# Two-buffered own rows and x rows in the second GCN edge stage of a four-layer graph network

## What is computed

```python
def gcn_conv(x, W, b, src, dst, n_nodes):      # src, dst with self-loops
    xw = x @ W
    deg = segment_sum(ones, dst)
    dis = rsqrt(deg)
    norm = dis[src] * dis[dst]
    return segment_sum(norm[:, None] * xw[src], dst) + b

h = relu(layernorm(x))
x = x + gcn_conv(relu(gcn_conv(h, W1, b1)), W2, b2)
h = relu(layernorm(x))                          # then the next layer
```

## Time and profile before

| | us |
|---|---|
| median of three runs | 5211.01 |
| lowest and highest run | 5206.4 and 5215.85 |
| profiled execution, its own time | 5226.53 |
| span of the profiled execution | 5224.8 |
| mean granted TensorE clock | 0.920 |
| busy in the span: TensorE / its weight loads | 75% / 63% |
| busy in the span: VectorE / GpSimd / ScalarE | 67% / 65% / 53% |

### The profile page before, as it was taken

The page is one execution under the profiler, slowest core; times in us unless marked ns, Lnnn a source line. Parts: engine busy times, 40 slices in busy tenths (PEclk is TensorE's granted clock), DMA queues, the critical chain, the costliest instruction groups (busy, mean ns, idle before and its releaser), DMA issues. The chain is left out here.

```text
span 5224.8 us, 117088 instructions
## 1 busy us (share of the span) xinstructions
PE 3910.9 (75%) x27481; PEld 3315.7 (63%) x27481; DVE 3497.0 (67%) x12527; ACT 2786.6 (53%) x7212; POOL 3413.1 (65%) x3998
## 2 busy tenths in 40 slices
PE   2888888888977698779999888665864966640176
PEld 1666666666866576778888777565764865640165
DVE  5888888886668766876666799327635833865433
ACT  2777777773434333656666688323522632430186
POOL 2666666665767576767567474575676667567577
PEclk9999999998988899999999999897997999875599
DMA  2776666664568676874334465794795788489443
GB/s 68 197 211 213 212 212 213 210 207 128 151 173 229 185 206 189 242 209 118 107 105 117 116 175 155 220 284 116 185 285 162 165 258 261 113 255 392 145 140 108
DMA packets 1087203, 971.64 MB, mean 186 GB/s; under 512 B 113214, under 2 KB 845974, under 8 KB 1087036
## 3 DMA queue, kind: packets, MB, share of 16 engines
q1 hardware_dynamic: 992956, 805.13, 50.6%
q0 software_dynamic: 94080, 164.48, 13.0%
HBM read 488.42 MB, written 484.70 MB: 186 GB/s over the span
## 5 line engine op out<-in xcount | busy, mean ns | idle before, releaser
L1093 POOL DMA_INDIRECT G<-table,idx_all x1568 | 1543.8, 985 | 758.8 <-issue 496.7
L1093 POOL DMA_INDIRECT G<-table,idx_l x588 | 603.8, 1027 | 291.5 <-issue 178.4
L1765 PE MATMUL PS<-G,S 128*128 (+1 forms) x2352 | 405.9, 290 | 27.8 <-DMA G<-table,idx_all 16.0
L1765 PE MATMUL PS<-CR,LO 97*128 97x128 f32 x2352 | 335.7, 288 | 67.8 <-ACT CR L2168 66.7
L1765 PEld LDWEIGHTS PS<-G,S 128*128 128x128 f32 x2352 | 351.0, 203 | 47.0 <-issue 29.0
L1765 PEld LDWEIGHTS PS<-S,G 128*128 128x128 f32 x1960 | 253.7, 195 | 168.2 <-issue 150.7
L1765 PEld LDWEIGHTS PS<-CR,LO 97*128 97x128 f32 x2352 | 303.6, 202 | 80.5 <-ACT CR L2168 79.5
L2168 ACT ACTIVATE G<-G 128x128 f32<-128x128 f32 x784 | 322.1, 483 | 60.4 <-issue 55.5
L1765 PE MATMUL PS<-S,G 128*128 128x128 f32 x1960 | 284.8, 287 | 92.6 <-DMA G<-table,idx_all 42.3
L1765 PE MATMUL PS<-G,FS 128*65 (+1 forms) x1764 | 276.4, 291 | 91.9 <-DMA G<-table,idx_all 52.8
L1765 PE MATMUL PS<-WX,OT 128*128 128x130 f32 (+1 forms) x2168 | 304.8, 285 | 36.9 <-ACT OT L2168 35.8
(11 more groups left out here) (381 smaller groups left out, 11146.4 us busy)
## 6 DMA issues: line engine op xcount, KB each, us to landing
table<-G SPq DMA_DIRECT2D x392, 256.0 KB, 3.4
table<-RO SPq DMA_DIRECT2D x271, 260.0 KB, 3.5
table<-RO SPq DMA_DIRECT2D x245, 256.0 KB
XIN<-xrows SPq DMA_DIRECT2D x196, 256.0 KB
table<-OWN SPq DMA_DIRECT2D x147, 260.0 KB
OWN<-table SPq DMA_DIRECT2D x139, 256.0 KB, 3.6
F<-table SPq DMA_DIRECT2D x132, 256.0 KB, 3.5
S<-table SPq DMA_DIRECT2D x100, 260.0 KB
```

What stands on the lines that cost most here:

```text
L1093: g.indirect_dma_start(G[:, t, 0:w], None, TAB[s], bass.IndirectOffsetOnAxis(ap=idx[:, t:t + 1], axis=0)).then_inc(gat[t % 4].sem, 16)
L1765: return nc.tensor.matmul(o, l, r, start=start, stop=stop)
```

## The change

In `C2` the product of own rows and `dis2` moves from VectorE to ScalarE (`scale_own`, four ACTIVATEs, one for each tile), two quads ahead. TensorE adds the scaled rows to the sums by four matmuls with the identity in `carries`. VectorE adds x to the sums straight from PSUM and drops the steps `own` and `comb`. x rows get a second buffer (`UT`, free in this stage) and are loaded two quads ahead; SP loads own rows after `agg` of the quad that used the buffer, in place of `comb`.

```diff
+        XINS = (XIN[:, :, :], rowwise(UT[:, :]))
...
-        scaled_own = steps("scaled_own", {"C1": ("own",)})
+        scaled_own = steps("scaled_own", {"C1": ("own",), "C2": ("own",)})
...
-            "C2": ("own", "comb", "x", "stats", "aggr", "rs", "nb"),
+            "C2": ("x", "stats", "aggr", "rs", "nb"),
...
                 def load_own(n, h):
-                    used, step = {"S1": (own_turned, "oT"), "C1": (agg, "t0"), "GZ": (agg, "t0")}.get(kind, (vd, "comb"))
+                    used, step = {"S1": (own_turned, "oT"), "C1": (agg, "t0"), "C2": (agg, "t0"), "GZ": (agg, "t0")}.get(kind, (vd, "comb"))
...
+                def load_x_h(n, h):
+                    if not isinstance(n, int) or n > 1:
+                        sp.wait_ge(vd.sem, vd.at(s, n - 2, "x"))
+                    else:
+                        sp.wait_ge(vd.sem, vd.at(s, 0))
+                    sp.dma_start(XINS[h], quad_rows(X_SRC[s], quad(n))).then_inc(xin_h[h].sem, 16)
...
                     if kind in own[h].order and at < LAST - 1:
                         load_own(n + 2, h)
+                    if kind == "C2" and at < LAST - 1:
+                        load_x_h(n + 2, h)
...
                 if kind == "C2":
-                    dve.wait_ge(own[h].sem, own[h].at(s, turn, "rows"))
-                    ins = v.tensor_tensor(own4, own4, wide(dis2[:, ds(Q4, 4)], D), ALU.mult)
-                    step(s, n, ins, "own")
                     aggregated(s, n)
-                    step(s, n, v.tensor_tensor(U4, A, own4, ALU.add), "comb", s3)
                     x_free(s, n, h, turn)
-                    step(s, n, v.tensor_tensor(XOUT[kind][h], U[:, :, :], XIN[:, :, :], ALU.add), "x", s2)
+                    step(s, n, v.tensor_tensor(XOUT[kind][h], A, XINS[h], ALU.add), "x", s3, s2)
...
-                if KINDS[s] == "GZ":
-                    pe.wait_ge(hself.sem, hself.at(s, n, "own"))
+                if KINDS[s] in ("C2", "GZ"):
+                    if KINDS[s] == "C2":
+                        pe.wait_ge(scaled_own.sem, scaled_own.at(s, n, "own"))
+                    else:
+                        pe.wait_ge(hself.sem, hself.at(s, n, "own"))
                     for i in (3, 2, 1, 0):
                         mm(sums_of(h, i), ident[:, :], OWNS[h][:, i, 0:D], False, False)
...
+            def scale_own(s, n, h, m):
+                Q4 = n * (-4) + 4 * LAST
+                act.wait_ge(own[h].sem, own[h].at(s, m, "rows"))
+                for j in range(4):
+                    row = OWNS[h][:, j, 0:D]
+                    i = f(row, row, ACT.Copy, scale=dis2[:, ds(Q4 + j, 1)])
+                i.then_inc(scaled_own.sem, 1)
...
                 if kind == "C2":
                     ahead(3, 2, 1)
+                    if not isinstance(n, int) or n < LAST - 1:
+                        scale_own(s, n + 2, h, m + 1)
                     sqrts(s, n)
                     ahead(0)
                     act.wait_ge(st_t.sem, st_t.at(s, n))
                     scaled(s, n, ACT.Relu, XOUT[kind][h])
...
+                if kind == "C2":
+                    scale_own(s, 0, 0, 0)
+                    scale_own(s, 1, 1, 0)
```

More of the change, by code:

```diff
@@ L328, in gnn_program @@
                      (QUADS + 1 - b) // 2) for b in (0, 1)]
-        xin = steps("xin", {k: ("rows",) for k in ("C2", "S2", "LB", "GZ")}, 16)
+        xin = steps("xin", {k: ("rows",) for k in ("S2", "LB", "GZ")}, 16)
         eas = steps("eas", {k: ("attr",) for k in ("LA", "LB")}, 16)
@@ L404, in gnn_program @@
         own_g = [Steps(sem(f"own_g{b}"), {"GA": ("rows",)}, 16, 0, KINDS, (QUADS + 3 - b) // 4) for b in range(4)]
+        xin_h = [Steps(sem(f"xin_h{b}"), {"C2": ("rows",)}, 16, 0, KINDS, (QUADS + 1 - b) // 2) for b in (0, 1)]
         st_g = [Steps(sem(f"st_g{b}"), {"GA": ("table",)}, 16, 0, KINDS, (QUADS + 1 - b) // 2) for b in (0, 1)]
@@ L966, in _ @@
                     load_own(1, 1)
+                if kind == "C2":
+                    load_x_h(0, 0)
+                    load_x_h(1, 1)
                 if kind in xin.order:
@@ L1580, in x_free @@
             def x_free(s, n, h, turn):
-                dve.wait_ge(xin.sem, xin.at(s, n, "rows"))
+                if KINDS[s] == "C2":
+                    dve.wait_ge(xin_h[h].sem, xin_h[h].at(s, turn, "rows"))
+                else:
+                    dve.wait_ge(xin.sem, xin.at(s, n, "rows"))
                 if not isinstance(n, int) or n > 1:
@@ L1906, in tile @@
                     else:
-                        used = "x" if kind == "GZ" else "comb"
+                        used = "comb" if kind == "S2" else "x"
                         pe.wait_ge(vd.sem, vd.at(s, n, used) - 2 * len(vd.order[kind]))
@@ L2396, in out_rows @@
                     f(RO[:, :, 0:D], bank(7), ACT.Copy).then_inc(ad.sem, 1)
[L2398 to L2404, removed]
                 def body_c1(n, h, m):
@@ L2412, in body_c1 @@
                     if among(n, 3):
-                        scale_own(n + 3, 1 - h, m + 1 + h)
+                        scale_own(s, n + 3, 1 - h, m + 1 + h)
                 def body_s1(n, h, m):
```

## The result

The changed kernel took **5317.43 us** in the median of four runs (5311.49 to 5319.91); the kernel before took 5210.2 beside it (four runs, 5206.4 to 5215.85). The ratio is **1.0202, 95% interval 1.0189 to 1.0215**: slower by 107 us. Forecast were 5326 us and a range of 5283 to 5375.

A forecast was written before the change was run, and what follows sets the result against it. VectorE's chain was taken to bound C2 at 5.88 us a quad; the changed loop takes 8.40. 46 quads give +115.9 us, start 1.9 later, last quads 2.4 saved: +115.4 on the median 5211.01, so 5326 us, range 5283 to 5375.

The forecast's parts named there:

- The ring: C2's closed chain per quad: GN store, own-rows load, four ACTIVATEs, root, norm, next store; forecast 8.40 us instead of 5.88.
- The fixed part, 4.60: Each C2 quad's loop without the load's landing: 0.02 and 0.84 to load issue, ACTIVATEs 1.28, root to norm 0.81, norm 1.65.
- L, 3.8: In C2, time from issue of the own-rows load to the start of the ACTIVATE waiting for it, taken as 3.8 us.
- the third rival: C2's own-rows load comes sooner as the longer quad thins traffic: L 2.85 to 3.4, about 5296 us; chance 0.11.
- the second rival: C2's own-rows load comes as late as the sage stage's x rows: L 4.2 to 4.86, about 5360 us; chance 0.15.
- The start: C2 up to quad 0's store: one load without a store ahead and eight more TensorE passes, 1.9 us later.
- The tail: C2's last two quads, which load nothing: without VectorE's L1594 and L1597 they save 2.4 us, at most 2.8.
- The sum: C2's total: 115.9 us for 46 quads, 1.9 later at the start, 2.4 saved at the end, together +115.4 us.
- What was to be seen: Signs in C2's changed profile: stores 8.0 to 8.8 us apart, VectorE below 50%, ScalarE waiting about 3.5 us a quad.
- Hidden after all: C2's own-rows load is hidden and GpSimd's gathers become the bound: 22 to 25 us saved, 5187 us; chance 0.06.
- TensorE as the bound: In C2, TensorE's eight added passes at a lower clock set the pace: about 5350 us, up to 5377; chance 0.08.

The follow-up runs named there:

- Run 1: Changed kernel, with SP issuing the load of own rows one turn earlier, ahead of the store of GN: 5208.35 us, 0.9945 of the kernel before.
- run 2: Changed kernel, SP's order kept, with ScalarE scaling the own rows behind the norm instead of ahead of its root: 5215.17 us, 0.9957 of the kernel before.
- run 5: Changed kernel, with SP issuing the load of own rows last in its turn, behind load and store of x: 5398.65 us, 1.035 of the kernel before.
- run 3: Changed kernel without TensorE's four identity matmuls in C2, own rows scaled but not added: 5334.54 us, 1.02 of the kernel before.
- run 8: Changed kernel with the two buffers of own rows exchanged, even quads into F, odd into OWN: 5319.73 us in one run.

## Why the prediction was right, and where its sizes were not

*The ring.* Right. The prediction said that a load with two quads of lead becomes a round trip inside each quad, since it stands in SP's order behind a store that waits for the norm. Run 1 takes that one thing away and the loss with it, and 0.55% more; run 2 cuts the ring at ScalarE and does the same; run 5 delays the load's issue by 1.18 us and its landing by 0.30, and the quad grows by 1.48.

*The fixed part, 4.60.* It measured 4.46: 8.20 less the mean landing of 3.74. The sum took the root to start when the ACTIVATEs end; in the rows it starts 0.10 before (1612.06 + 1.28 = 1613.34 against 1613.24). The sum took 0.84 from store to load, the mean of two rows; over the 46 quads it is 0.79. From root to norm it is 0.81 in the mean, as in the sum, and 0.02 and 1.65 for the norm hold within 0.01. 46 x 0.14 = 6.4 us of the forecast's surplus are this.

*L, 3.8.* The mean over the 46 loads was 3.74, so the term was right in sum, but it is two sizes: 4.08 for the 28 loads that landed while gathers ran, 3.22 for the 18 behind them. Store to store that is 8.54 and 7.66 us. One of the later landings and its use:

```profile
1751.28 0.39 SPq L872 DMA_DIRECT2D F<-table  x1
...
1754.51 1.28 ACT L2184 ACTIVATE F<-F,dis 128x128 f32<-128x128 f32 x4 [4.07 <-DMA F<-table]
```

3.23 us here. Behind the gathers the loads came as the third rival had it, sooner (2.85 to 3.4); beside them a sooner one and one as late as the second rival had it (4.2 to 4.86) came in turn, 3.36 and 4.83 in the median. That the flat 3.8 met the mean of these is in part luck. The prediction itself said that the gathers would end halfway; it should have made two terms of it. By the Trainium skill's fit, "DMA: Bandwidth & Descriptors", section "Anatomy of one DMA", L was estimated at 2.6 us; no load of the 46 landed in under 2.8. The fit is for DMAs that GpSimd issues, and these are SP's.

*Start and tail.* The start was +2.4 us for +1.9. The tail is the step that failed: -0.65 for -2.4. Without a load in the last two quads VectorE's two steps were taken to be the path that shrinks; in the changed kernel two other waits of ScalarE stand there, for quad 47 and for quad 48:

```profile
1875.14 0.27 ACT L2184 ACTIVATE CR<-PS 1x128 f32<-1x128 f32 x1 [1.44 <-PE PS L1778]
...
1879.45 1.65 ACT L2184 ACTIVATE GN<-RB,nb,rs 128x128 f32<-128x128 f32 x4 [1.48 <-DMA table<-GN]
```

The first is for TensorE's sums of the next quad, ahead of the norm; the second is for the store of the norm before, out of the one `GN` buffer. In the kernel before neither wait stands at these places. No run took one of them away, so how the 1.75 us divide between them is not shown.

*The sum.* 106.6 + 2.4 - 0.65 = 108.35 in the stage, against 115.4; the medians differ by 107.2. Of the 7 us too much, 6.4 are the fixed part and 46 x 0.06 = 2.8 the landing; the start (0.5) and the tail (1.75) were off in the other direction, so that the total is closer than its parts.

*What was to be seen.* Stores 8.0 to 8.8 us apart: 8.20 in the mean, though single quads took 7.15 to 9.57. VectorE below 50%: 45. Load 0.7 to 1.0 behind the store: 0.69 and 0.97. Gathers ending as early: yes. ScalarE's wait "about 3.5 us a quad" was wrong, 4.40, and by the prediction's own terms: from the end of the norm the load takes 0.86 + L, and the copy `CR` covers 0.25 of it, which is 4.41 with L = 3.8.

*The rivals.* Hidden after all (0.06): not in this kernel, but run 1 shows that its price was sound. 0.9945 of 5211 is 5182, where 5187 was forecast, and the stage ends 13 us behind its last gather, as it said (13 to 16). TensorE as the bound (0.08): excluded by run 3. The rule of the Trainium skill, "Trainium Kernel Development and Optimization", section "Best Practices", to double-buffer so that DMA overlaps compute, does not hold here by the two buffers alone: with them the ratio is 1.0202 in one order of issue and 0.9945 in another. What agrees with both is a rule of the Trainium skill, "DMA: Bandwidth & Descriptors", section "Rules for kernel authors": issue the DMA early and wait on its semaphore late. Run 1 does the first, run 2 the second, and either is enough.

## What to carry to other kernels

A second buffer hides a load only if the load can be *issued* early. Follow its queue: if a store ahead of it waits for the engine that will use the load, and that engine waits for the load ahead of the work that feeds the store, a lead of two quads shrinks to one round trip of issue, landing and use. Before a wait is moved ahead on an engine, look for what is queued behind it there and whether the awaited transfer hangs on that; here, putting the load ahead of the store turned +2.0% into -0.55%.

## What was not expected of the hardware

While gathers ran, loads of the same 256 KB from the same queue landed in turn early and late, 3.36 and 4.83 us in the median; behind the gathers they took 3.12 and 3.16. Which of the two buffers was the late one changed from kernel to kernel (runs 3 and 8) and within run 8, and what sets it is open.

The granted clock was 0.84 in a steady 100 us of the kernel before, 0.71 in the changed one, whose TensorE waits in every quad for `CR` and in most for the scaled rows, 0.65 in run 3, and 1.00 in run 1, where those waits are fewer and shorter (16.7 us in 24 for `CR` in 1500 to 1720, 0.2 in one for the scaled rows): a mix of the two levels, 1.2 and 2.4 GHz, in the first three, the upper one alone in the last. A steady 100 us of run 1:

```profile
1560.00:1660.00 100.00, 78.53 (x599) 68.34 (x597) 71.44 (x324) 67.75 (x211) 75.16 (x77) 1.00 0.88 250
```

TensorE did 599 instructions there in 78.53 us, where the changed kernel did 363 in 71.81: much of its busy time in the changed kernel was the lower clock. Nothing here shows that it cost the changed kernel time: in run 3, with fewer passes and a lower clock still, the waits for the load and the ratio were the same.
